# Causal attention with q projected head dimension first, its halves exchanged by ScalarE

## The reference

```python
h = _rmsnorm(hidden_states, ln1_w)
q = _rope((h @ Wq).reshape(B, S, NH, HD), pos)
k = _rope((h @ Wk).reshape(B, S, KVH, HD), pos)
v = (h @ Wv).reshape(B, S, KVH, HD)
scores = einsum('bqhd,bkhd->bhqk', q, repeat(k, 8)) / sqrt(HD)
attn = softmax(where(causal, scores, -1e9))
o = einsum('bhqk,bkhd->bqhd', attn, repeat(v, 8)).reshape(B, S, NH * HD) @ Wo
# _rope: x1, x2 are the halves of a head's 128 numbers
# [x1 * cos - x2 * sin, x1 * sin + x2 * cos]
```

## Time and profile before

| | us |
|---|---|
| median of 3 runs | 1177.41 (1174.01 to 1184.52) |
| the profiled execution: its time | 1178.93 |
| the profiled execution: its span | 1177.1 |
| PE busy | 1065.7 (91% of the span) |
| DVE, ACT, POOL busy | 814.2, 632.4, 591.4 |

### The profile page before, as it was taken

How to read it: one execution, slowest core, us unless ns; L and a number is a source line. 1 busy time by engine, 2 the same in 40 slices (tenths; PEclk the granted TensorE clock), 3 DMA queues, 4 the chain that set the end, 5 groups by cost and what they waited for, 6 DMA issues and landing times. The chain is left out here.

```text
span 1177.1 us, 22288 instructions
## 1 busy us (share of the span) xinstructions
PE 1065.7 (91%) x6799; PEld 924.7 (79%) x6799; DVE 814.2 (69%) x1988; ACT 632.4 (54%) x1899; POOL 591.4 (50%) x624
## 2 busy tenths in 40 slices
PE   3897888797799659999999999999979999999998
PEld 2676777586455349998999899999978888888887
DVE  7665575625888768788788788888876555555555
ACT  3454553425799636665666567666654333434342
POOL 5243121541777555664565467554534555555553
PEclk9788997798799879999999999999998999999999
DMA  8000000000324020020002000000011111111111
GB/s 248 1 1 1 1 18 1 16 1 25 120 78 147 12 80 2 2 82 2 3 2 82 3 2 2 2 1 1 2 30 34 47 43 50 41 52 40 53 40 50
DMA packets 44099, 41.74 MB, mean 35 GB/s; under 512 B 6161, under 2 KB 40049, under 8 KB 44001
## 3 DMA queue, kind: packets, MB, share of 16 engines
q1 hardware_dynamic: 42384, 39.54, 10.8%
q10 hardware_dynamic: 1616, 0.99, 0.3%
HBM read 39.40 MB, written 1.11 MB: 34 GB/s over the span
## 5 line engine op out<-in xcount | busy, mean ns | idle before, releaser
L2153 POOL TENSOR_TENSOR hid_l<-hid,hid_h 128x512 fp32r<-128x512 f32 x66 | 85.5, 1295 | 134.0 <-ACT hid_h L2122 134.0
L1760 POOL TENSOR_TENSOR qr<-r_part_a,r_part_b 128x512 f32<-128x512 f32 x64 | 82.4, 1287 | 118.0 <-DVE r_part_b L1805 117.9
L1774 POOL TENSOR_TENSOR prob<-prob,rden 128x128 f32<-128x128 f32 (+1 forms) x256 | 123.9, 508 | 22.9 <-DVE rden L1856 22.5
L2180 DVE TENSOR_TENSOR hid<-psum,silu 128x512 f32<-128x512 f32 x66 | 45.6, 691 | 125.1 <-ACT silu L2120 125.0
L1720 ACT ACTIVATE prob<-psum,neg_max 128x128 f32<-128x128 f32 (+1 forms) x256 | 105.3, 418 | 37.0 <-DVE neg_max L1845 30.2
L2172 DVE SCALAR_TENSOR_TENSOR x<-psum,weight,x 128x256 f32<-128x256 f32 x264 | 108.9, 475 | 0.0
L73 PE MATMUL psum<-xt_h,gu_l 128*128 128x512 f32 x264 | 105.9, 401 | 0.6 <-DVE xt_l L160 0.6
L75 PE MATMUL psum<-xt_h,gu_h 128*128 128x512 f32 x264 | 104.7, 397 | 0.0
L74 PE MATMUL psum<-xt_l,gu_h 128*128 128x512 f32 x264 | 104.3, 395 | 0.0
L2120 ACT ACTIVATE silu<-psum 128x512 f32<-128x512 f32 x66 | 39.4, 597 | 115.7 <-PE psum L75 115.7
L1296 POOL TENSOR_TENSOR drive<-u,b_all 128x1024 f32<-128x1024 f32 x32 | 75.5, 2362 | 42.3 <-DVE h L1412 20.8
(11 more groups left out here) (279 smaller groups left out, 3613.7 us busy)
## 6 DMA issues: line engine op xcount, KB each, us to landing
b_all<-scan_b_rows SPq DMA_DIRECT2D x16, 512.0 KB, 3.8
early<-in_L_ffn_Wq_dram SPq DMA_DIRECT2D x4, 1024.0 KB, 5.1
early<-in_L_ffn_Wo_dram SPq DMA_DIRECT2D x4, 1024.0 KB, 7.5
raw<-in_L_ffn_Wg_dram SPq DMA_DIRECT2D x32, 128.0 KB, 2.1
raw<-in_L_ffn_Wu_dram SPq DMA_DIRECT2D x32, 128.0 KB, 2.3
raw<-in_L_ffn_Wd_dram SPq DMA_DIRECT2D x32, 128.0 KB, 2.3
x<-_attn_hidden_states_dram SPq DMA_DIRECT2D x8, 128.0 KB, 4.9
early<-in_L_ffn_w_up_q_dram SPq DMA_DIRECT2D x1, 1024.0 KB, 7.4
```

Source lines behind the costliest of these rows:

```text
L1760: pool.tensor_tensor(qr[:, i, :], part_a[:, slot, :], part_b[:, slot, :], ALU.add).then_inc(roped, 1)
L1774: ins = pool.tensor_tensor(at, at, rden[:, s % 4, i:i + 1].to_broadcast([P, (i + 1) * P]), ALU.mult)
L2153: pool.tensor_tensor(hid_l[:, j, cols], hid[:, c, :], f(hid_h[:, j, cols]), ALU.subtract)\
```

## The change

The q projection exchanges its operands: 128 columns of q weights (one head) are stationary and the 256 tokens of a batch move, so a bank holds two heads with a head's numbers on the partitions and the tokens along the free axis. Twelve matmuls of 256 columns take the place of six of 512. The four transposes of `turn_q` are gone, and so are `q_0` and its copy: the scores read `qr` directly, and `split_q` makes the high and low parts of the last 128 tokens, on ScalarE from SBUF and on GpSimd (VectorE before).

For the rotation the halves of a head now lie on different partitions. ScalarE has a new part `q` behind each projection: two copies of 64 partitions x 512 out of PSUM, each into the other half of `r_part_b`. VectorE waits for both, multiplies PSUM by cos into `r_part_a`, and then `r_part_b`, in place and now in SBUF, by sin, in one instruction of 512. GpSimd's addition is as before. The tables of cos and sin for q are turned once by four transposes at the layer's start and scaled out of PSUM.

`split_q` stands at r = 5, 6 and 1, 2. The split q weights have one buffer where there were two; the pieces come as kv, o, q, the q pieces at steps 21, 23, 25, 27 of a group (`WHEN`), the first piece of either half of the q weights waiting for the last projection that reads the old ones. The raw q weights are loaded by a DMA of their own, and the loop on SP is written out. One semaphore counts VectorE's own writes in all norms.

```diff
-        wq_h, wq_l = (sb(f"wq_{n}", [P, 2 * KD, REP1 * HD1], F32R) for n in "hl")
+        wq_h, wq_l = (sb(f"wq_{n}", [P, KD, REP1 * HD1], F32R) for n in "hl")
         wkv_h, wkv_l = (sb(f"wkv_{n}", [P, 2 * KD, 2 * HD1], F32R) for n in "hl")
         wo_h, wo_l = (sb(f"wo1_{n}", [P, 2 * REP1, D], F32R) for n in "hl")
-        tables = sb("rope1", [P, 2, 2, 2, HD1], F32)
+        tables = sb("rope1", [P, 2, 2, HD1], F32)
+        q_tables = sb("rope1_q", [P, 2, S], F32)
...
-        qr = sb("qr", [P, 2, QC], F32)
+        qr = sb("qr", [P, 2, QB, S], F32)
         kr = sb("kr", [P, 2, HD1], F32)
 
 
-        q_0 = sb("q1_0", [P, 2, QB, P], F32)
...
+        WHEN = dict(zip((6, 8, 10, 12, 14, 21, 23, 25, 27), KV + O + Q))
...
-                    yield "turn_q", gg, 2 * b + 1, r - 1
+                    yield "split_q", gg, 2 * b + 1, r - 1
                 if more and r == 5:
                     yield "turn_k", *ahead_b(gg, b + 1)
-                if more and r in (6, 7):
-                    yield "turn_q", *ahead(gg, 2 * b + 2), r - 6
+                if more and r in (5, 6):
+                    yield "split_q", *ahead(gg, 2 * b + 2), r - 5
...
-                if not last and 6 <= s < 6 + 2 * PIECES and s % 2 == 0:
-                    yield "weights", gg + 1, (s - 6) // 2
-
-        FIRST = [("kv", 0, 0), ("q", 0, 0, 0), ("q", 0, 0, 1), ("turn_k", 0, 0), ("turn_q", 0, 0, 0),
-                 ("turn_q", 0, 0, 1), ("norm_rest",), ("q", 0, 1, 0), ("q", 0, 1, 1), ("scores", 0, 0), ("peak", 0, 0)]
+                if not last and s in WHEN:
+                    yield "weights", gg + 1, *WHEN[s]
...
-                def turn_q(g, m, c):
-                    act.wait_ge(qk_turned, turn_index(g, m, c) + 1)
-                    bank = psum[:, TURNB, :].rearrange("p (h t n) -> p h t n", h=2, t=2)
-                    act.activation(q_0[:, m % 2, 2 * c:2 * c + 2, :], bank[:, :, 0, :], ACT.Copy).then_inc(first_out, 1)
-                    act.activation(q_h[:, m % 2, 2 * c:2 * c + 2, :], bank[:, :, 1, :], ACT.Copy).then_inc(qk_hi, 1)
+                def q(g, m, i):
+                    index = q_index(g, m, i)
+                    act.wait_ge(projected, index + 1)
+                    if not known(index, 2):
+                        act.wait_ge(roped, index - 1)
+                    for c in range(2):
+                        lo, hi = slice(c * HD1 // 2, (c + 1) * HD1 // 2), slice((1 - c) * HD1 // 2, (2 - c) * HD1 // 2)
+                        ins = act.activation(part_b[lo, q_index(0, m, i) % 2, :], psum[hi, PROJB[i], :], ACT.Copy)
+                    ins.then_inc(q_swapped, 1)
+
+                def split_q(g, m, i):
+                    act.wait_ge(roped, q_index(g, m, i) + 1)
+                    at = slice(2 * i, 2 * i + 2)
+                    act.activation(q_h[:, m % 2, at, :], qr[:, m % 2, at, P:S], ACT.Copy).then_inc(q_hi, 1)
...
-                    before = turn_index(g, m - 1, 1) if m else k_turn_index(g, 0) - 1
-                    if not known(before, 0):
-                        pool.wait_ge(qk_turned, before + 1)
                     slot = q_index(0, m, i) % 2
-                    pool.tensor_tensor(qr[:, i, :], part_a[:, slot, :], part_b[:, slot, :], ALU.add).then_inc(roped, 1)
+                    pool.tensor_tensor(qr[:, m % 2, 2 * i:2 * i + 2, :].rearrange("p h n -> p (h n)"), part_a[:, slot, :],
+                                       part_b[:, slot, :], ALU.add).then_inc(roped, 1)
+
+                def split_q(g, m, i):
+                    pool.wait_ge(q_hi, q_order(g, m, i) + 1)
+                    at = slice(2 * i, 2 * i + 2)
+                    pool.tensor_tensor(q_l[:, m % 2, at, :], qr[:, m % 2, at, P:S], f(q_h[:, m % 2, at, :]),
+                                       ALU.subtract).then_inc(q_lo, 1)
...
+                dve.wait_ge(tables_turned, 1)
+                dve.tensor_scalar(q_tables[:], psum[:, TURNB, :].rearrange("p (a n) -> p a n", a=2), HD1 ** -0.5, None,
+                                  ALU.mult).then_inc(tables_own, 1)
...
-                    rope(q_index(0, m, i) % 2, psum[:, PROJB[i], :].rearrange("p (h n) -> p h n", h=QB), 0, i, QB)\
-                        .then_inc(parts, 1)
+                    slot = q_index(0, m, i) % 2
+                    src, a, b = (x.rearrange("p (h n) -> p h n", h=2)
+                                 for x in (psum[:, PROJB[i], :], part_a[:, slot, :], part_b[:, slot, :]))
+                    cos, sin = (q_tables[:, n:n + 1, :].to_broadcast([P, 2, S]) for n in range(2))
+                    dve.wait_ge(q_swapped, q_order(g, m, i) + 1)
+                    dve.tensor_tensor(a, src, cos, ALU.mult)
+                    dve.tensor_tensor(b, b, sin, ALU.mult).then_inc(parts, 1)
...
+                pe.wait_ge(loaded_c, 16 * 4)
+                for n, table in enumerate((tables[:, 0], tables[:, 1])):
+                    for t in range(2):
+                        ins = pe.transpose(psum[:, TURNB, n * S + t * P:n * S + (t + 1) * P], table[:, t, :], core.ident[:])
+                ins.then_inc(tables_turned, 1)
...
-                    for k in range(KD):
-                        where = ds((g & 1) * KD + k, 1)
-                        cols = slice((m % 2) * QC, (m % 2 + 1) * QC)
-                        ins = product(pe, bank, core.xt(k, slice(b * S + i * P, b * S + (i + 1) * P)),
-                                      (wq_h[:, where, cols], wq_l[:, where, cols]), k == 0, k == KD - 1)
+                    for j in range(2):
+                        head = m % 2 * QB + 2 * i + j
+                        for k in range(KD):
+                            cols = slice(head * HD1, (head + 1) * HD1)
+                            ins = product(pe, bank[:, j * S:(j + 1) * S], (wq_h[:, k, cols], wq_l[:, k, cols]),
+                                          core.xt(k, slice(b * S, (b + 1) * S)), k == 0, k == KD - 1)
...
-                def turn_q(g, m, c):
-                    index = turn_index(g, m, c)
-                    pe.wait_ge(roped, q_index(g, m, 1) + 1)
-                    pe.wait_ge(qk_lo, index)
-                    for hh in range(2):
-                        for i in range(2):
-                            head = 2 * c + hh
-                            ins = pe.transpose(psum[:, TURNB, hh * S + i * P:hh * S + (i + 1) * P],
-                                               qr[:, i, head * HD1:(head + 1) * HD1], core.ident[:])
-                    ins.then_inc(qk_turned, 1)
...
-                    pe.matmul(first, q_0[:, m % 2, h % QB, :], k_0[:, b % 2, :], start=True, stop=True,
+                    pe.matmul(first, qr[:, m % 2, h % QB, 0:P], k_0[:, b % 2, :], start=True, stop=True,
```

More of the change, by code:

```diff
@@ L102, in begin @@
     def begin(self, dve):
-        self.count = Count(dve, self.own)
+        self.count = self.c.dve_count
+        self.count.eng = dve
         self.scale = self.rs if self.twice is None else self.rs2
@@ L1795, in norm_rest @@
                     norm.low(dve, 1)
-                def rope(slot, src, kind, t, heads):
-                    cos, sin = ((tables[:, kind, n, t:t + 1, :] if t is not None else tables[:, kind, n, :, :])
-                                .to_broadcast([P, heads, HD1]) for n in range(2))
-                    a, b = (x[:, slot, 0:heads * HD1].rearrange("p (h n) -> p h n", h=heads) for x in (part_a, part_b))
-                    dve.tensor_tensor(a, src, cos, ALU.mult)
-                    for c in range(2):
-                        lo, hi = slice(c * HD1 // 2, (c + 1) * HD1 // 2), slice((1 - c) * HD1 // 2, (2 - c) * HD1 // 2)
-                        ins = dve.tensor_tensor(b[:, :, lo], src[:, :, hi], sin[:, :, lo], ALU.mult)
-                    return ins
                 def q(g, m, i):
@@ L1989, in norm_rest @@
                     norm.tensor(pe, (1,))
[L1991 removed]
+                run(pe, dict(q=q, kv=kv, turn_k=turn_k, scores=scores, turn_probs=turn_probs,
                              values=values, project_out=project_out, norm_rest=norm_rest))
```

150 lines of the change are left out of this document (83 added, 67 removed).

## The result

| | before | after |
|---|---|---|
| median us | 1176.88 (4 runs, 1174.01 to 1184.52) | 1204.89 (4 runs, 1201.57 to 1208.13) |
| profiled execution, its span | 1178.93, 1177.1 | 1201.57, 1199.7 |
| PE, ScalarE busy in the span | 1065.7, 632.4 | 1048.3, 684.8 |

The changed kernel takes 1.0211 times as long (95% interval 1.0175 to 1.0248). PE works 17 us less and the kernel is 28 us slower. The two traces are 22.6 us apart, and the last scores start 22.95 us later (863.92, now 886.87): the time was lost in the attention layer before them. The traced execution is the fastest of the changed kernel's four; the 5.4 us between 22.6 and 28.0 can't be read from a trace.

The account below looks back on a forecast made before the run. PE was taken to bound the attention layer, busy 49.63 of 50 us. From the profiled 1178.9, adding 14.7 (PE's waits), 5.4 (weight pieces) and 1.3 (start) gave 1200.3, or 1198.8 against the median; forecast 1199, range 1166 to 1216.

Parts of the forecast that it names:

- case A: The favoured outcome, chance 0.48: slower as worked out, 1199 us, its own range 1189 to 1209.
- The ring: Projection, exchange, rotation, reciprocal, `pt_l`: PE waits for this chain at r=1 and r=6; +0.98 us a batch, +14.7 in all.
- PE's own work: Without `turn_q` each of 64 pieces gives back 0.42 us, 27 in all; a projecting step is then 3.62.
- The exchange: ScalarE's two copies behind each q projection: 1.08 us, bounds 0.67 and 1.30, ending at +1.28 after the scores' start.
- the start: Head of the attention layer: eight z instructions, then two exchanges, rotation and maxima; about +1.3 us, bounds -4 and +4.
- The exp behind the exchange: On ScalarE the next exp queues behind the copies but ends near +2.15, before VectorE wants it; no cost counted.
- The slack of 0.04 in the long steps: At r=3 and 4 PE reaches the next transposes at +4.20, the chain at +4.16, so the chain is hidden.
- GpSimd beside the sin: Weight pieces delay GpSimd, whose SBUF work makes VectorE's sin multiplication wait 0.6 us at nine places: +5.4, bounds 0 and 36.
- D: Rival, chance 0.08: GpSimd is late at every sin, each of 60 projections costs 0.6 us; 1229 us.
- B: Rival, chance 0.14: faster, the exchange is cheap or runs beside other work and PE's shorter list shows; 1151 us.
- C: Rival, chance 0.20: no difference, the exchange at its lower bound 0.67 and weight pieces hide more; 1182 us.
- E: Rival, chance 0.10: PE's waits of 1.4 to 2.0 us lower the granted clock at one in three of 30; +17, 1216.

Follow-up runs that it names:

- The idle copies: Against the changed kernel: VectorE rotates q with halves unexchanged, while ScalarE still makes two 64x512 copies, from the table to an unread tile; 1195.47 us, ratio 1.0133 to before.

## Why the prediction was right

1199 was forecast, 1204.9 measured, inside the range and inside case A's own. The ring is what happens: `pt_l` releases PE at r=1 and r=6, with 1.06 and 1.01 idle where 1.1 to 1.5 was named as the sign, and 1.4 and 1.6 in the working (part of it has moved ahead, into r=0 and r=5, now 2.48 and 2.58 for 2.19 and 2.42); PE's share fell to 90%; ScalarE rose to 37.4 in 50 us (39 foretold); the batch grew by 1.38 for 0.98.

- **PE's own work**: right. The long steps are 3.63, foretold 3.62; the gain shows in r=7 and r=2 and in the kernel without the exchange, 1157.
- **The exchange**: mis-sized. Two copies from first start to last end: 1.20, foretold 1.08. The overlap of 0.11 was taken from two copies of 256 columns; here a third copy starts 0.10 before the second ends, but the two together show none of it against 2 x 0.593. VectorE follows 0.13 after the end, not 0.04. Together 0.20, which puts `pt_l` at +3.80 for +3.59 and PE at +4.36 for +4.16; two waits x 0.20 is the 0.40 that the batch is longer than foretold. That 0.20 is the step that failed, in size and not in kind. By the traces 21.4 was foretold and 22.95 came: the ring 19.3 in 14 batches for 14.7 in 15 (the first lies in the start), the pieces 3.4 for 5.4, the start 1.8 for 1.3, the turns of the loop -1.6 where nothing was foretold. That the sums agree so well is in part luck: these errors cancel, and the -1.6 is a clock that happened to stay up at one turn. The median is 5.9 above the forecast.
- **VectorE's rotation** from cos to reciprocal: 1.21, foretold 1.22. **The reciprocal to `pt_l`**: 1.06, and 1.05 in before.
- **The exp behind the exchange**: counted as covered, which it is as long as VectorE waits too. The idle copies showed that it would carry 2.1 of the 2.6 us a batch alone. The sentence was right for the sum; what it hides is that taking away VectorE's wait alone would have given back 0.6.
- **The slack of 0.04 in the long steps**: gone, as the +4.36 says (0.14 lost), without a price of its own, since the ring carries it on.
- **GpSimd beside the sin**: the mechanism and the number of places, nine, were right, the price is 0.46 each and 4.1 in all, for 0.6 and 5.4. ScalarE's half of a piece, which the prediction left out, costs 1.7. That the net is 3.4 comes from two smaller things: before has 0.8 of its own in such batches (27.10 for 27.01), and the chain without a piece in the way is 4.26 in groups with pieces and 4.35 in the last one, which stays unexplained. The Trainium skill (page "SBUF — State Buffer", SBUF: two separate sides) has the VectorE instruction with two inputs in SBUF and the GpSimd instruction that reads SBUF exclude each other for the whole instruction. The trace agrees: the sin took 1.15 beside a multiplication of 0.99 and 1.35 beside an addition of 1.26, and ended 0.55 after GpSimd both times. It was not the bound (D).
- **The start**: +1.8 for +1.3, bounds -4 to +4. The z instructions began 3.9 earlier, not 2.5, the two exchanges took 2.42, not 2.2, and one sin of 1.35 is in it; the near hit is a sum of misses.
- **The rivals**: B and C needed a cheaper copy: 64 partitions cost 593 ns where 128 cost 597. E didn't come: the granted clock is 1.00 in the windows of 50 us with the ring's waits, up to 1.4 us (600 to 650 and 800 to 850). It fell at one of the two turns of the loop, where before lost it at both.

## What to carry to other kernels

An operation taken off the bounding engine pays only if the chain that replaces it fits into the shortest step behind it, so write out the lengths of the steps one by one: the loss here comes from the two of eight that follow a projection and hold none. The cure wasn't a cheaper operation but another place: the same rotation ahead of a step with 3.6 us of PE's work costs 0.1 to 0.2 (steps of 3.70 to 3.84 for 3.63), ahead of one with 2.2 it costs 1.4 more (2.86 us a batch for two of them). When something is moved, move its consumers too, and look what it now stands in front of and what stands in front of it.
